# Loading the next step's table words in the middle of a step, on the queues of VectorE and ScalarE

## The reference, cut to what matters

```python
def _gat_layer(x, src, dst, ea, W, We, a_src, a_dst, a_edge, b, n):
    h = x @ W
    e = ea @ We
    s = (h @ a_src)[src] + (h @ a_dst)[dst] + e @ a_edge
    s = jax.nn.leaky_relu(s, NEG_SLOPE_ATT)
    smax = jax.ops.segment_max(s, dst, num_segments=n)
    ex = jnp.exp(s - jax.lax.stop_gradient(smax)[dst])
    denom = jax.ops.segment_sum(ex, dst, num_segments=n)
    alpha = ex / denom[dst]
    out = jax.ops.segment_sum(h[src] * alpha[:, None], dst, num_segments=n)
    return out + b
...
for i in range(MID):          # layers 1 to 3
    c = _gat_layer(h, ...)
    beta = math.log(THETA / (i + 1) + 1.0)
    h = (1.0 - ALPHA) * c + ALPHA * x0
    h = (1.0 - beta) * h + beta * (h @ mid_ws[i])
    h = jax.nn.leaky_relu(h, 0.01)
```

## Time and profile before

| | |
|---|---|
| median of three runs | 13,679.91 us |
| the profiled execution | 13,686.51 us, span 13,684.8 us |
| mean granted TensorE clock | 0.837 of 2.4 GHz |
| busy: PE / PEld | 9,345.4 us (68%) / 8,215.7 us (60%) |
| busy: VectorE (DVE) | 8,876.7 us (65%) |
| busy: ScalarE (ACT) | 6,472.5 us (47%) |
| busy: GpSimd (POOL) | 9,449.1 us (69%) |

### The profile page before, as it was taken

How to read it: one execution, slowest core, us unless ns; L and a number is a source line. 1 busy time by engine, 2 the same in 40 slices (tenths; PEclk the granted TensorE clock), 3 DMA queues, 4 the chain that set the end, 5 groups by cost and what they waited for, 6 DMA issues and landing times. The chain is left out here.

```text
span 13684.8 us, 304796 instructions
## 1 busy us (share of the span) xinstructions
PE 9345.4 (68%) x64194; PEld 8215.7 (60%) x64195; DVE 8876.7 (65%) x23089; ACT 6472.5 (47%) x12901; POOL 9449.1 (69%) x10337
## 2 busy tenths in 40 slices
PE   6888886666666666666666666666665555657999
PEld 6888885555555555555555555555554555554699
DVE  4667776666776666776666776666775444446787
ACT  5555664444444444444444444444444222225887
POOL 3777776777775777775777775777774777773266
PEclk7878887888888888888888888888887778788999
DMA  4222222222222222222222222222222444446754
GB/s 101 54 54 54 54 54 49 54 54 54 54 56 49 54 54 54 54 56 48 54 54 54 54 56 57 54 54 54 54 53 52 108 110 112 115 117 201 220 147 136
DMA packets 905699, 1019.87 MB, mean 75 GB/s; under 512 B 535592, under 2 KB 589063, under 8 KB 905482
## 3 DMA queue, kind: packets, MB, share of 16 engines
q0 software_dynamic: 300288, 630.00, 21.3%
q1 hardware_dynamic: 517362, 256.23, 7.7%
q10 hardware_dynamic: 87848, 131.57, 2.8%
HBM read 875.68 MB, written 142.21 MB: 74 GB/s over the span
## 5 line engine op out<-in xcount | busy, mean ns | idle before, releaser
L969 POOL DMA_INDIRECT rows<-node_table,idx x9384 | 8883.7, 947 | 3363.9 <-issue 2924.7
L1200 PE MATMUL bank<-ident,u_edge 128*128 128x128 f32 x8800 | 2145.1, 323 | 3182.8 <-DVE u_edge L1061 3177.4
L1200 PEld LDWEIGHTS bank<-ident,u_edge 128*128 128x128 f32 x8800 | 1380.3, 157 | 3768.3 <-DVE u_edge L1061 2735.9
L1234 PE MATMUL bank<-rows,work 128*128 x17600 | 3011.9, 326 | 33.1 <-ACT work L1319 19.1
L1234 PEld LDWEIGHTS bank<-rows,work 128*128 128x128 f32 x17600 | 2765.9, 239 | 104.1 <-issue 100.3
L1300 ACT ACTIVATE work<-bank,v_low 128x512 f32<-128x512 f32 x2200 | 1511.8, 687 | 2542.6 <-PE bank L1202 1940.3
L1074 DVE SCALAR_TENSOR_TENSOR work<-bank,acc,work 128x512 f32<-128x512 f32 x1760 | 1321.1, 751 | 1601.1 <-issue 1593.3
L1202 PE MATMUL bank<-mask_ident,other_lane 128*128 128x128 bf16 x8800 | 1898.1, 244 | 0.0
L1081 DVE TENSOR_REDUCE group_top<-work 128x1 f32<-128x512 f32 x2200 | 1508.4, 686 | 271.4
L1213 PE MATMUL bank<-ident,work 128*128 128x128 f32 x8800 | 1654.3, 321 | 0.0
L1056 DVE SCALAR_TENSOR_TENSOR other_lane<-bank,group_base,dst_of 128x512 bf16<-128x512 f32 x2200 | 1632.0, 742 | 9.9 <-issue 5.5
(11 more groups left out here) (283 smaller groups left out, 11846.1 us busy)
## 6 DMA issues: line engine op xcount, KB each, us to landing
rows<-edge_features SPq DMA_DIRECT2D x831, 256.0 KB, 2.8
rows<-node_table,idx POOLq DMA_INDIRECT x9384
edge_features<-work ACTq DMA_DIRECT2D x440, 256.0 KB
work<-in_edge_attr SPq DMA_DIRECT2D x48, 256.0 KB, 3.3
node_table<-acc ACTq DMA_DIRECT2D x147, 65.0 KB
idx<-sources_by_quad SPq DMA_DIRECT2D x150, 32.0 KB
node_table<-hx SPq DMA_DIRECT2D x7, 458.5 KB, 4.4
node_table<-hx SPq DMA_DIRECT2D x1, 3209.5 KB, 22.2
```

The lines of the kernel that those rows point to most:

```text
L969: nc.gpsimd.indirect_dma_start(rows[:, s, q * TW:(q + 1) * TW], None, tables[layer % 2], bass.IndirectOffsetOnAxis(ap=idx[:, half, s, q:q ...
L1200: nc.tensor.matmul(bank[r][:, q * P:(q + 1) * P], u_edge[:, r, q:q + 1].broadcast_to([P, P]), ident[:, :], start=True, stop=False, is_tran ...
L1234: ins = nc.tensor.matmul(bank[4 + r][:, 0:P + 1], att[:, r, q * P:(q + 1) * P], rows[:, at(slot), q * TW:q * TW + P + 1].rearrange("p a w ...
```

## The change

VectorE's and ScalarE's `fetch` no longer load their row at the start of each step. A new `fetch_ahead` loads the row of step j+1 in step j: on VectorE between the issue of the row maximum (L1081) and the wait for it, on ScalarE behind the issue of `exps`. It does so in seven steps of eight: in the last step of a turn (`k` is 7) nothing is loaded ahead, and the first step of the next turn loads at its start as before. A step at whose predecessor the stage is not live also loads at its start. The number of loads stays. Layer 4's second load in ScalarE's `fetch` stays where it is.

```diff
@@ staged_pipeline
-        begin(turn * unroll + k)
+        begin(turn * unroll + k, k)
@@ VectorE
-                def fetch(j):
+                def words_for(j):
+                    return group_words(dve, j + 2, 0, 4 if first else 5)
+
+                def fetch_ahead(j, k):
+
+                    if k != UN - 1:
+                        now["ahead"] = words_for(j + 1)
+
+                def fetch(j, k):
 
                     if isinstance(j, int) and j + 2 >= ROWS - 4:
                         return
-                    words = group_words(dve, j + 2, 0, 4 if first else 5)
+                    words = now.pop("ahead", None) if k else None
+                    if words is None:
+                        words = words_for(j)
...
-                    c.link(nc.vector.reduce_max(group_top[:, r, :], sloped[:, r, :], AX.X))
+                    top = nc.vector.reduce_max(group_top[:, r, :], sloped[:, r, :], AX.X)
+                    fetch_ahead(i, k)
+                    c.link(top)
@@ TensorE
-                staged_pipeline(pe, UN, stages, lambda j: None)
+                staged_pipeline(pe, UN, stages, lambda j, k: None)
@@ ScalarE
-                def fetch(j):
+                def words_for(j):
+                    return group_words(act, j + 3, 2, 3 if first else 6)
+
+                def fetch_ahead(j, k):
+
+                    if k != UN - 1:
+                        now["ahead"] = words_for(j + 1)
+
+                def fetch(j, k):
                     if isinstance(j, int) and j + 3 >= ROWS:
                         return
-                    words = group_words(act, j + 3, 2, 3 if first else 6)
+                    words = now.pop("ahead", None) if k else None
+                    if words is None:
+                        words = words_for(j)
...
                     nc.scalar.activation(att_t[:, r, :], sloped[:, r, :], ACT.Exp, bias=neg_now[:, r, :])\
                         .then_inc(att_t_made, 1)
+                    fetch_ahead(i, k)
```

## The result

The changed kernel takes 13,634.15 us (median of 7 runs, 13,627.69 to 13,641.64), against 13,683.18 for seven runs of the kernel before on the same chip: ratio 0.9964 [0.9955, 0.9974]. That is 49 us less where 60 were forecast. The profiled execution took 13,641.64 us, span 13,639.9.

What follows compares the result with a forecast made beforehand. The prediction took GpSimd's gathers to bound the kernel, with gains only at layers' ends: 14 + 12 + 12 + 19 + 1.5 + 1 = 60 us off 13,680 gives 13,620, range 13,597 to 13,662.

Steps and rivals of the forecast that it cites:

- The bound: GpSimd gathers without a stop, 1.25 us each; a faster VectorE step pays only in the waits at layers' ends.
- Removed and added: VectorE's tail step: 0.78 us of idle removed, 0.43 added at the reduction, net 0.35, times 7/8: 0.31.
- rival B: VectorE's load starts only when L1081 has ended, costing 1.03 us instead of 0.43: +31 us, 13,711; chance 0.08.
- The net of 0.31 us a step: VectorE's tail steps: net saving after the factor 7/8; over 42 steps 13 us in each of layers 1 to 3.
- Layer 4: Tail of layer 4: 0.49 us a step, times 7/8 times 42 is 18; with the start 19 us.
- rival A: In the tails the 5.15 us path to the next step's `bend` takes over: 22 us gained, 13,658; chance 0.15.
- rival C: Code reloading at loop ends: 4 turns of 3 us in three layers take back 36 us, 13,656; chance 0.08.
- Layers 1 to 3: the step that failed: Tails of layers 1 to 3: the change shortens the waits after them by 14, 12 and 12 us.
- the small term of 2 us each for `bend`: Tails of layers 2 and 3: at low clock `bend` waits on a 5.15 us path and gives back 2 us each.
- The 5.15 us of the earlier trace: Path from L1061 through logits, weighing and mixing to L1349, read as its length at 1.2 GHz, longer than a 4.7 us step.
- ScalarE, cost 0: ScalarE's load moved behind `exps`: covered by `copy_turned`'s 1.3 us wait for TensorE, so cost 0 and gain 0.
- the sum: Whole kernel: 14 + 12 + 12 + 19 + 1.5 + 1 = 60 us; by the net's bounds 36 to 76.

Runs made afterwards that it cites:

- ends_only_b: The change in layers 0 and 4 alone, layers 1 to 3 loading as before; against the kernel before: 13,647.42 us, ratio 0.9983.
- after_b: The changed kernel run again, on a chip as fast as the first; against the kernel before: 13,627.49 us, ratio 0.9968.
- dve_only_b: VectorE's part of the change alone, ScalarE loading at each step's start as before; against the kernel before: 13,639.93 us, ratio 0.9976.
- warm_b: The changed kernel with six TensorE transposes of the identity per step in layers' tails; against the kernel before: 13,578.80 us, ratio 0.9933.
- split_warm: The changed kernel with the six transposes and each long load cut in two, on a slower chip; against the kernel before: 17,079.84 us, ratio 0.9980.

## Why the prediction was right and where it was not

**The bound.** Right on the faster chips. GpSimd's stream did not speed up with VectorE's step (VectorE waited for arrivals instead, 154.1 us against 31.5), and what the change gave a layer, it gave in the wait at its end. On the slower chips it does not hold, as told above.

**Removed and added.** Right in mechanism and size. L1126's idle is gone except at a turn's first step; L1095 starts 0.97 us after L1091 with the short load and 1.57 to 1.67 with the long one (medians of the tails; forecast 0.96 and 1.56). So the load does run beside the reduction, and rival B fell. The net of 0.31 us a step is 0.29 measured at full clock on the slower chips, 0.27 on the faster ones.

**Layer 4.** 21.1, 24.3, 24.0 and 23.5 us in four profiles where 19 were forecast. Layer 4 has neither `mix_rows` nor `bend`, so the path of rival A isn't in it, and A's "half in layer 4" had no ground. The 3 us stalls at loop ends stayed (longest 3.6 us), and none came to layers 1 to 3 (longest 1.1): rival C fell too.

**Layers 1 to 3: the step that failed.** It is the sentence against rival A, "the clock there is 0.90, so mostly full, and a denser TensorE has no reason to get less", and with it the small term of 2 us each for `bend`. Two things in the sentence were wrong. First, before's tails are not a fixed 0.97, 0.90, 0.91: the same steps in ends_only_b had 0.88, 0.93, 0.91, so layer 1's full clock, on which its 14 us rested, was a good draw. Second, TensorE is not denser in every step. Of the nine tails with changed steps (after, after_b, dve_only_b) the mean granted clock is 0.862, of the six with unchanged steps (before, ends_only_b) 0.917. At like clocks the change is worth about 0.2 us a step over the whole tail: unchanged 5.21 us at 0.88 and 5.15 to 5.17 at 0.90 and 0.91, changed 5.02 at 0.88 and 4.94 at 0.91. But from 0.91 to 0.83 a changed step grows from 4.94 to 5.18 us, 0.03 for each 0.01, and the mean fall of 0.055 takes back 0.16 of the 0.2. In the mean over these tails a step is 5.10 changed and 5.13 unchanged, and a wait 90.0 against 94.1 us: 4 us a layer, where 12 to 14 were forecast. So rival A had the right place, the wait of `bend` for L1349 (now L1372). It came in layer 1 as well, and where I had priced it by the clock as it was, the clock moved as well. Two readings behind that price were off too. The 5.15 us of the earlier trace rows are not the path at the low clock: of that stretch 3.4 us were at 1.2 GHz and the rest at 2.4, so at the low clock throughout it would be longer. And `bend` waited for L1349 in 8 and 7 of layers 2 and 3's tail steps, not in every second one.

Why the clock falls is shown in part. That the pauses have to do with it, warm_b shows: it puts work into them, and the clock is 0.99 to 1.00. That it is the alternation of short and long steps, rather than the changed place of the work, was meant to be tried with split_warm; since the split load was not shorter, it stays argued. The fall itself holds only for a mean over tails that each scatter by 0.03.

**ScalarE, cost 0.** On the faster chip dve_only_b, without ScalarE's part, is 12 us slower than after_b, 0.08% with intervals that overlap: no cost shows there. dve_only_b's profile had gathers of 947 ns against 944, but that execution took 13,660.0 us, 20 more than the median of its runs, so the 12 us can't be put down to the gathers. On the slower chips ScalarE's part alone cost 0.2 to 0.3%; there "cost 0" failed, and the runs don't show in which step.

**What the sum left out.** Of after's 45 us in the profiles, about 17 are gathers: some 3 us in each of six passes (five layers and the edge features) at 945 instead of 947 ns; at 944 it is 22. Only 26.7 us are waits, where the terms of the sum for the four waits were 57. after_b's waits are 42.8 us below before's profile, so the change itself is worth some 27 to 43 us by the profiles. How the 49 and 45 us of the medians divide is open: with which of the two times the kernel before ran in them, no profile shows. If it was 947 throughout, 17 to 22 us of them are the gathers' and the forecast of 60 was about twice what the change brought; if it was 944 or 945, the forecast was a quarter to a third too high. That the median came within 11 us of the forecast may thus be luck in part.

## What to carry to other kernels

A load into registers can be hidden beside a long instruction of its own engine, behind its issue and ahead of the wait for it; price it by the mean over long and short loads. Before putting a saved step time into a sum, follow the second path that starts in the same step, and take its length at the lower granted clock: where it is longer than the new step, the change has to shorten both, or keep TensorE at work, to pay in full. And profile a kernel more than once before a clock of one stage becomes a term: here the same tail had 0.97 and 0.88. Ask of every chip anew which stage bounds it, before a ratio measured there is read as that of one stage.

## What the runs showed of the hardware

- The gather on GpSimd takes 944, 945 or 947 ns in the mean over 9,384, the same through a whole profiled execution, and the same kernel had 944 in one and 947 in another. The busy time differs by up to 22 us, 0.16% of this kernel.
- The kernel before takes 13.7 ms on some chips and 17.1 to 17.3 on three. There TensorE, VectorE and ScalarE stand idle together for over 1 us 82 to 100 times in the middle of a layer, and GpSimd waits 3.4 to 3.7 ms for free slots.
- Six 128-column transposes a step that compute nothing took the granted clock of three tails from 0.84 to 0.92 (after_b) up to 0.99 to 1.00 (warm_b), and the kernel from 0.9968 to 0.9933 of the time before. On the slower chips the same transposes on the unchanged kernel gave 0.9995 and 0.9997, no change clear of noise.
- A `TENSOR_LOAD` on VectorE's queue took 590 or 1190 ns for five words, by turns from one row of 24 bytes to the next, at the start of a step (before) as beside the reduction (after; there the long one took up to 1,360 in the tails); one on ScalarE's 310 or 920 for four.
